# Cross-attention in a decoder kernel: the weighted sums of two quarters of heads in one block, with four probability buffers

## What is computed

```
x = x + self_attention(layernorm(x))             # 16 heads of 64
x = x + cross_attention(layernorm(x), context)   # 16 heads of 16, context 361 rows per batch
x = x + experts(layernorm(x))                    # each token goes to one of 8 experts
```

```
q = x Wq.T + bq;  k = context Wk.T + bk;  v = context Wv.T + bv
scores = q k.T / 4, masked;  attn = softmax(scores);  out = (attn v) Wo.T + bo
```

## Time and profile before

| | |
|---|---|
| time, median of 3 runs | 1566.71 us (1562.39 to 1567.07) |
| the profiled execution's own time | 1566.04 us |
| its span, first to last instruction | 1564.3 us |
| granted TensorE clock, mean over the span | 0.967 of full speed |
| PE busy | 1434.1 us, 92% of the span |
| DVE busy | 967.4 us, 62% |
| ACT busy | 763.7 us, 49% |
| POOL busy | 682.0 us, 44% |
| weighted sums (L1677), PE | 3072 instructions, from 693.4 to 1217.0 us |
| row maxima (L1431), DVE | 512, 530 ns each |
| exponentials (L1305), ACT | 384, 507 ns each |
| first load of expert weights issued (L1864) | at 1243.78 us |

### The profile page before, as it was taken

One profiled execution on the slowest core, in us unless ns is written; L12 is line 12 of the kernel. 1 busy time (PEld: TensorE's weight loads), 2 busy tenths in 40 slices (PEclk: granted clock), 3 DMA queues, 4 the chain that ended last, 5 costly groups with the idle time before them and its releaser, 6 DMA issues. The chain is left out here.

```text
span 1564.3 us, 40213 instructions
## 1 busy us (share of the span) xinstructions
PE 1434.1 (92%) x12305; PEld 1241.7 (79%) x12305; DVE 967.4 (62%) x2473; ACT 763.7 (49%) x1879; POOL 682.0 (44%) x1060
## 2 busy tenths in 40 slices
PE   4999999999999999789999999999999369999997
PEld 3888878888888888668888888888887258888886
DVE  5747575757565656357777777777775235555553
ACT  4647474747464656236655655655655112222221
POOL 5434353535353535512355455465464523333332
PEclk9999999999999999789999999999999579999999
DMA  5606060707070707077667767767764235554451
GB/s 191 136 5 167 20 172 13 179 9 181 8 177 11 173 12 176 26 217 194 193 176 198 194 178 195 194 176 196 195 168 141 69 110 166 197 194 169 160 191 54
DMA packets 181964, 218.31 MB, mean 140 GB/s; under 512 B 83838, under 2 KB 150309, under 8 KB 181638
## 3 DMA queue, kind: packets, MB, share of 16 engines
q1 hardware_dynamic: 176360, 208.56, 48.1%
q0 software_dynamic: 3968, 6.59, 1.3%
q10 hardware_dynamic: 1568, 2.30, 0.5%
HBM read 138.67 MB, written 80.48 MB: 140 GB/s over the span
## 5 line engine op out<-in xcount | busy, mean ns | idle before, releaser
L1431 DVE TENSOR_REDUCE row_max<-psb_s 100x1 f32<-100x361 f32 x512 | 265.3, 530 | 140.1 <-PE psb_s L1654 135.0
L1305 ACT ACTIVATE probs<-psb_t 121x400 f32<-121x400 f32 (+1 forms) x384 | 190.4, 507 | 89.7 <-PE psb_t L1664 82.8
L1654 PE MATMUL psb_s<-k,q 97*100 97x362 f32 x512 | 185.0, 363 | 12.8 <-DVE row_max L1431 4.9
L519 POOL TENSOR_TENSOR diag<-neg_ident,row_max 100x400 fp32r<-100x400 f32 x128 | 112.8, 903 | 175.5 <-DVE row_max L612 146.7
L1664 PE MATMUL psb_t<-q,k 98*121 98x200 f32 (+1 forms) x768 | 148.5, 276 | 1.8 <-ACT probs L1305 1.8
L2144 PE MATMUL psd_h<-h_in,w_sb 128*128 128x256 f32 x640 | 144.0, 384 | 1.4 <-ACT h_in L2010 1.4
L2152 PE MATMUL psd_y<-w_sb,hid 128*128 128x256 f32 x640 | 144.5, 379 | 0.0
L2144 PEld LDWEIGHTS psd_h<-h_in,w_sb 128*128 128x128 f32 x640 | 123.3, 193 | 18.9 <-issue 1.8
L2152 PEld LDWEIGHTS psd_y<-w_sb,hid 128*128 128x128 f32 x640 | 120.1, 190 | 15.5
L1664 PEld LDWEIGHTS psb_t<-q,k 98*121 98x121 f32 (+1 forms) x768 | 126.8, 186 | 5.6 <-ACT probs L1305 2.5
L2025 ACT ACTIVATE hid<-psd_h,b_sb 128x256 f32<-128x256 f32 x100 | 47.4, 474 | 148.5 <-PE psd_h L2144 147.2
(11 more groups left out here) (230 smaller groups left out, 3710.0 us busy)
## 6 DMA issues: line engine op xcount, KB each, us to landing
w_sb<-in_w SPq DMA_DIRECT2D x40, 1024.0 KB, 7.6
routed_rows<-empty SPq DMA_DIRECT2D x7, 3855.0 KB, 18.7
packed_keys<-k_st SPq DMA_DIRECT2D x32, 724.0 KB, 4.1
k<-packed_keys SPq DMA_DIRECT2D x64, 362.0 KB
v_rows<-v_tok SPq DMA_DIRECT2D x32, 400.0 KB
v_ext<-v_rows SPq DMA_DIRECT2D x32, 400.0 KB
q<-packed_queries SPq DMA_DIRECT2D x64, 200.0 KB
k<-packed_keys SPq DMA_DIRECT2D x64, 181.0 KB
```

Source lines behind the costliest of these rows:

```text
L519: pool.tensor_tensor(diag[:, g % 2], c.neg_ident[0:S, 0:S].unsqueeze(1).to_broadcast([S, GH, S]), row_max[:, g // 2 % 2, g % 2].unsqueeze( ...
L1305: act.activation(probs[0:KT[kt], u % 2, kt], ps_t[i % 2][0:KT[kt], 0:4 * S], ACT.Exp, scale=HD2 ** -0.5).then_inc(probs_ready, 1)
L1431: dve.reduce_max(row_max[:, p, h:h + 1], ps_s[h % 2][0:S, 0:S2], AX_X).then_inc(max_ready, 1)
L1654: pe.matmul(ps_s[h % 2][0:S, 0:S2E], q2[0:97, p, u, g, S * a:S * (a + 1)], k2[0:97, p, u, g], start=True, stop=True).then_inc(scores_ready, 1)
```

## The change

The four blocks of weighted sums in an iteration become two of two quarters each. Quarters 2 and 3 of batch b-1 stand together where quarter 3 stood (behind the turned maxima, before score 3). Quarters 0 and 1 of batch b stand together behind the turned sums and before shifted 2,0. So weighted 2 moves from between scores 14 and 15 into the next iteration, weighted 0 from before the routing to behind score 7 and the turned sums, and weighted 1 from behind score 10 forward to the same place. The probabilities get four buffers, one for each quarter; the two new ones lie in the memory of the expert tables `b2_sb` and `cen`, so SP loads these two tables only after the last weighted sum. The number of matmuls, their shapes, and the work of ACT, DVE and POOL stay as they were.

```diff
-        probs = sb("probs2", [KP, 2, 3, 4 * S])
+        probs_01 = sb("probs2", [KP, 2, 3, 4 * S])
+        probs = [probs_01[:, 0], probs_01[:, 1]] + [t[0:KP].rearrange("p e d -> p (e d)")[:, 0:3 * 4 * S].rearrange(
+            "p (k n) -> p k n", k=3) for t in (c.b2_sb, c.cen)]
...
+            sp.wait_ge(pv_ready, B * 4)
             for dst, src in ((c.cen, moe["centroids"]), (c.b2_sb, moe["b2"])):
...
             def exps(b, u, kt):
                 if kt == 0:
-                    reach(act, pv_ready, b * 4 + (u - 1))
+                    reach(act, pv_ready, b * 4 + (u - 3))
...
-                act.activation(probs[0:KT[kt], u % 2, kt], ps_t[i % 2][0:KT[kt], 0:4 * S], ACT.Exp,
+                act.activation(probs[u][0:KT[kt], kt], ps_t[i % 2][0:KT[kt], 0:4 * S], ACT.Exp,
...
-                                        probs[0:n, u % 2, kt, S * h:S * (h + 1)], start=(kt == 0), stop=(kt == 2))
+                                        probs[u][0:n, kt, S * h:S * (h + 1)], start=(kt == 0), stop=(kt == 2))
...
                 if not first:
-                    weighted(b - 1, 1 - p, 3)
+                    for u in (2, 3):
+                        weighted(b - 1, 1 - p, u)
                 maximum_of(3)
...
                 maximum_of(6)
-                weighted(b, p, 0)
                 if exists(b, RT):
                     routing(b, p)
                 maximum_of(7)
                 if not first:
                     turn_raw(b - 1)
+                for u in (0, 1):
+                    weighted(b, p, u)
                 shifted(b, p, 2, 0)
...
                 maximum_of(10)
-                weighted(b, p, 1)
                 if not first:
                     turn_out(b - 1)
...
                 maximum_of(14)
-                weighted(b, p, 2)
                 maximum_of(15)
 
             over_batches(pe, step)
             routing(B, 0)
-            weighted(B - 1, 1, 3)
+            for u in (2, 3):
+                weighted(B - 1, 1, u)
```

## The result

The changed kernel takes 1579.11 us (median of 4 runs, 1577.41 to 1581.14) against 1566.36 us before in the same comparison: 12.8 us slower, ratio 1.0092 with a 95% interval of 1.0076 to 1.0107. The forecast was 1575 us, 1560 to 1584. The granted clock, a mean over the span, differs a little between executions and moves the time with it (the kernel before took some 1570 us at 0.964 of full speed and 1561 at 0.973). At 0.972 and 0.973 the changed kernel took 1578.4 and 1577.4 us, the kernel before, in the comparisons further down, 1559.4 to 1562.8 (11 executions), so that at an equal clock the loss is some 16 us.

What follows compares the result with a forecast made beforehand. PE, 98.9% busy, was taken as the bound. Per iteration -0.69 on PE, +0.73 POOL, +0.25 DVE, +0.05 weight load make +0.34 us; 29 times gives +9.9, less 1.2: 1566.7 + 8.7 = 1575 us, range 1560 to 1584.

Steps and rivals of the forecast that it cites:

- The sign: Whole kernel: the change makes it slower, by 8.7 us; slower was given a chance of 0.64.
- the two waits: First keys matmul waits for POOL, +0.73 us an iteration; score 7 waits for DVE, +0.25 us; both together 0.50.
- Weighted 2 leaves its place, POOL holds the keys matmul: Values 2 to keys: of 0.85 us freed on PE only 0.12 is had; POOL's chain needs 3.15 us.
- DVE holds score 7: Score 3 to score 7: maximum 5 allows no less than 2.81 us, so score 7 waits +0.25 us.
- Weighted 2 in front of weighted 3: Joint block before score 3: 24 more starts of 20.4 ns add 0.49 us, with no new entry or exit.
- The joint block behind the turned sums: Weighted 0 and 1 between turned sums and shifted 2,0: 1.14 us plus 0.05 for the hand-over, +1.19 us an iteration.
- The 1.2 us put down for the last batches: Last two or three iterations: no keys wait, about 0.4 us kept each, the last bound by ACT; -1.2 us.
- Weighted 1 out of its place: Score 10 to the turned quotients: 0.16 us where 0.92 stood, -0.76 us an iteration.
- the keys matmul's own load: Keys matmul that waits loses its weight load's overlap: 0 to 0.1 us, taken as +0.05 us an iteration.
- The buffers and the late tables at nothing: Two new probability buffers and the later load of `cen` and `b2_sb` cost no time.
- mode changes decide: Keys matmul not held by POOL's split: PE's own -0.69 us an iteration holds, 1545 us, or 1553 with DVE's wait; chance 0.16.

Runs made afterwards that it cites:

- run 10: Kernel before with weighted 2 alone moved, to weighted 3, and POOL's context split in halves with keys matmuls reordered: 1556.88 us, ratio 0.9968.
- run 2: Kernel before with the new buffers and weighted 2 alone moved, to weighted 3; weighted 0 and 1 in their old places: 1573.95 us, ratio 1.0057.
- run 5: Changed kernel with DVE's statistics of batch b+3 behind maximum 7 instead of between maxima 4 and 5: 1569.48 us, ratio 1.0021 to the kernel before.
- run 9: Kernel before with the new buffers and only weighted 0 and 1 joined, between routing and score 7; POOL's split whole: 1555.17 us, ratio 0.9949.
- run 1: Changed kernel with the weighted blocks back in their old places, four buffers and later table load kept: 1565.37 us, ratio 1.0007 to the kernel before.
- run 8: Changed kernel with weighted 0 and 1 before score 7, POOL's context split in halves and keys matmuls reordered: 1550.89 us, ratio 0.9901 to the kernel before.
- run 6: Changed kernel with the joint block of weighted 0 and 1 between the routing and score 7: 1564.07 us, ratio 0.9995 to the kernel before.
- run 4: Changed kernel with the second part of POOL's context split in halves and keys matmuls reordered: 1562.88 us, ratio 0.9992 to the kernel before.
- run 11: As run 8, with the first half's maxima turned ahead of shifted 2,1 and score 9, and ACT's copy moved earlier: 1549.68 us, ratio 0.9897.
- run 12: As run 8, with PE's 32 iterations written out instead of looping over two at a time: 1552.93 us, ratio 0.9930 to the kernel before.

## Why the prediction was right

The sign, the two waits and their places were right; the size was 0.2 us an iteration short, and that the time came as near as it did is in part luck (see the fourth point).

- *Weighted 2 leaves its place, POOL holds the keys matmul.* Right: 3.15 us forecast, 3.14 measured, with the wait in the waits view, and run 10 shows that the move gains once POOL is quicker. This is the greater cost: 0.43 us alone (run 2).
- *DVE holds score 7.* Right: 2.81 us forecast, 2.82 measured. Without the statistics it is 2.48 (run 5), so the wait is 0.34 and not 0.25 us. The forecast took 2.55 = 3.31 - 0.76 for PE alone; but score 6 follows score 3 after 1.60 instead of 1.70 us, because ACT issues its transfer earlier there (run 9). The hand-over to the routing, 0.24 instead of 0.16 us, and the routing itself, 0.04 us shorter, take back 0.04 of that.
- *Weighted 2 in front of weighted 3.* +0.52 us measured, +0.49 forecast. The 24 starts come in six groups of four (7 ns apart within a group), one group every 86 to 90 ns. The forecast's 20.4 ns a start is their average within one block; six groups of 86 ns give the 0.52.
- *The joint block behind the turned sums.* This term was mis-sized: +1.19 us forecast, +1.38 measured (0.87 to 2.25). The turned sums hand over after 0.53 us instead of 0.36, an entry of 0.17 us where the sum had 0.05 and the bound 0.10, and the block holds 1.17 instead of 1.14 us. The score ahead and the shifted pair behind it take 0.02 us more each. This term makes up the whole of the missing 0.2 us, which over 29 iterations is 5.8 us. The medians show 4.1 us of it. The 1.2 us put down for the last batches as given back were not seen: in the profiles at full clock these batches took 1.2 us more. The clock hid the difference: the four changed executions had a mean clock of 0.969 to 0.973, the profiled one before had 0.967, and at an equal clock the loss is some 16 us, not 12.8.
- *Weighted 1 out of its place, the keys matmul's own load.* Within 0.04 us each (-0.80 us for -0.76, +0.06 for +0.05).
- *The buffers and the late tables at nothing.* Right (run 1).
- *The rival "mode changes decide"* was right that joining blocks saves time on PE: run 8, with both waits out of the way, gains 0.50 of its 0.69 us an iteration, and run 10 gains 0.19 with one joint block. In the changed kernel the waits took more than that. The rule of the Trainium skill on draining at a change of tiling mode (TensorEngine Tiling (Array Packing), Key Properties) agrees with a block of 0.65 us for 0.47 us of starts; whether a drain saved shortens anything is another matter, and here it did only once the waits were out of the way.

## What to carry to other kernels

When one engine is 99% busy, ask of each piece of its work what it covers before moving it: another engine's chain (here POOL's 3.15 us, 0.12 us from late) or a slow reply (here maximum 5, 2.8 us behind score 3). Read that slack as the distance between the start that triggers the chain and the start that needs it, in the trace, and compare it with the chain's own length; the wait views show nothing of it until it is used up. A batch of work for a full engine should go where something else is being waited for: the same joint block cost 0.08 us an iteration behind score 7 and gained 0.27 in front of it.

## What the runs showed of the hardware

- What it costs to enter a block of four matmuls side by side depends on what stands ahead of it: 0.16 us from the last, very short routing matmul (run 6), 0.26 from a score (before; 0.33 from score 6 in run 2), and 0.53 instead of 0.36 us from four transposes of 128 columns (after). Why the last is dearest isn't settled.
- A turn of the hardware loop costs PE's sequencer a median of 208 ns for the branch that jumps back and 76 ns for the last one, which doesn't (both kernels and runs 4, 8 and 11), against a median of 45 ns on ACT (run 11). With only scores 14 and 15 ahead of it, the next matmul is 0.17 us late (0.33 instead of 0.16, run 11); with weighted 2 and score 15 ahead of it, not at all (before). Written out, the loop brought the late transfer of run 12 instead; its cause isn't shown.
- Issuing one DMA of 3.1 KB from ACT's list holds that list for 0.64 us (runs 6 and 9), and an exponential behind it starts that much later: a cost on an engine that is 60% busy, which PE pays through a PSUM bank.
